# One tile instead of four in the engine loop of two delta-rule layers, with single buffers and three copies by ScalarE

## The reference, cut to what matters

```python
q = softmax(q, axis=-1); k = softmax(k, axis=-1); beta = sigmoid(beta)
def step(W, inp):                     # W: (4, 8, 32, 32), zero at first
    qt, kt, vt, bt = inp
    wk    = einsum('bhde,bhe->bhd', W, kt)
    v_new = bt * (vt - wk)
    W     = W + einsum('bhd,bhe->bhde', v_new, kt)
    return W, einsum('bhde,bhe->bhd', W, qt)
```

## Time and profile before

| | |
|---|---|
| median of three runs | 5422.78 us |
| the profiled execution, device time | 5467.1 us |
| its span | 5465.3 us |
| TensorE busy in the span | 4194.9 us (77%) |
| mean granted TensorE clock | 0.82 of full speed |
| fast-weight layer 0, M updates of its loop (L847) | 542.6 to 1125.9 us |

### The profile page before, as it was taken

One profiled execution on the slowest core, in us unless ns is written; L12 is line 12 of the kernel. 1 busy time (PEld: TensorE's weight loads), 2 busy tenths in 40 slices (PEclk: granted clock), 3 DMA queues, 4 the chain that ended last, 5 costly groups with the idle time before them and its releaser, 6 DMA issues. The chain is left out here.

```text
span 5465.3 us, 173116 instructions
## 1 busy us (share of the span) xinstructions
PE 4194.9 (77%) x75148; PEld 2525.7 (46%) x75149; DVE 2689.1 (49%) x5011; ACT 1812.7 (33%) x3259; POOL 877.7 (16%) x2195
## 2 busy tenths in 40 slices
PE   3666666667986666666788887699999999984995
PEld 1235455453435555554245554255454544533663
DVE  3443223233023323332478887378685886852343
ACT  1121111112121111110366665167575775731221
POOL 0000000000000000000155554011111111104012
PEclk7776666667996666666899998799999999995997
DMA  1000000000000000000100000000000000005123
GB/s 41 2 8 4 4 4 4 4 4 18 0 6 4 4 4 4 4 4 5 37 1 1 1 1 1 9 1 0 1 0 1 0 1 1 0 3 210 61 83 101
DMA packets 47696, 88.13 MB, mean 16 GB/s; under 512 B 7120, under 2 KB 38128, under 8 KB 46064
## 3 DMA queue, kind: packets, MB, share of 16 engines
q1 hardware_dynamic: 40944, 61.84, 3.3%
q0 software_dynamic: 6144, 16.79, 0.9%
HBM read 45.05 MB, written 33.55 MB: 14 GB/s over the span
## 5 line engine op out<-in xcount | busy, mean ns | idle before, releaser
L1618 PE MATMUL psum<-hm_ex,hm_mix 128*128 128x512 f32 x1024 | 510.4, 621 | 42.2 <-ACT hm_Aq L1698 38.2
L1684 ACT ACTIVATE hm_ex<-psum,hm_nm 128x1024 f32<-128x1024 f32 x256 | 285.5, 1115 | 297.6 <-DVE hm_nm L1742 297.6
L1752 DVE TENSOR_SCALAR_CACHE_REDUCE hm_plus<-hm_Aq,hm_cbcol,hm_sums 128x1024 f32<-128x1024 f32 x256 | 340.4, 1330 | 0.0
L1618 PEld LDWEIGHTS psum<-hm_ex,hm_mix 128*128 128x128 f32 x1024 | 175.5, 191 | 352.2 <-issue 344.5
L1757 DVE COPY hm_A<-psum 128x1024 f32<-128x1024 f32 x256 | 312.8, 1222 | 51.5 <-PE psum L1627 47.8
L1742 DVE TENSOR_REDUCE hm_nm<-psum 128x1 f32<-128x1024 f32 x256 | 310.9, 1215 | 13.3 <-PE psum L1606 13.3
L1627 PEld LDWEIGHTS psum<-K,hm_Aq 128*128 128x128 f32 x2048 | 236.7, 140 | 149.9 <-issue 145.2
L666 PE MATMUL psum<-fw_w,fw_stage 128*128 128x512 f32 (+1 forms) x512 | 286.8, 697 | 17.7 <-DMA fw_w<-in_slow 16.6
L1689 ACT ACTIVATE hm_junk<-hm_Aq 128x1024 f32<-128x1024 f32 x256 | 270.6, 1057 | 30.3
L1606 PE MATMUL psum<-hm_kt,hm_qd 64*32 64x512 f32 x4096 | 279.8, 605 | 0.0
L1627 PE MATMUL psum<-K,hm_Aq 128*128 128x128 f32 x2048 | 266.6, 273 | 5.6 <-DVE hm_A L1757 5.6
(11 more groups left out here) (360 smaller groups left out, 8207.4 us busy)
## 6 DMA issues: line engine op xcount, KB each, us to landing
ex_rows_in<-ex_zero SPq DMA_DIRECT2D x2, 5120.0 KB, 24.5
ex_xs<-ex_rows_in SPq DMA_DIRECT2D x80, 128.0 KB
ex_rows_out<-ex_ys SPq DMA_DIRECT2D x80, 128.0 KB, 1.7
ex_w<-in_ex_w SPq DMA_DIRECT2D x2, 4096.0 KB
X<-in_x SPq DMA_DIRECT2D x2, 2048.0 KB, 11.0
out_y<-X SPq DMA_DIRECT2D x2, 2048.0 KB, 9.0
ff_w<-in_ff_w SPq DMA_DIRECT2D x2, 1024.0 KB, 5.9
pt_w_proc<-in_pt_proc SPq DMA_DIRECT2D x1, 2048.0 KB, 7.7
```

What stands on the lines that cost most here:

```text
L1618: mm = pe.matmul(bank[4 + c], mix[:, u, :], ex[:, u, 512 * c:512 * c + 512], start=True, stop=True)
L1684: act.activation(ex[:, u, :], flat2(psum[:, 2 * u:2 * u + 2, :]), ACT.Exp, bias=nm[:, u:u + 1], accum_out=rsum[:, u:u + 1]).then_inc(s_ex, 1)
L1752: dve.tensor_scalar(plus[:, :], Aq[:, u, :], cbcol[:, :], sums[:, :], ALU.add, ALU.add, accum_out=sums[:, :]).then_inc(s_run, 1)
```

## The change

The loop passes from four bodies to one: the bodies -1 to 1 are written out, a loop runs the bodies 2 to 30 (29 passes), and the bodies 31 and 32 follow. So that one body fits every tile, each array has a single buffer. Where the next tile overwrites an array before the recurrence of the tile before has read it, ScalarE copies it: `vhc` from `vh`, `qkTc` from `qkT`, `kc` from the key half of `qk`. The recurrence reads the copies. Several waits are added so that no buffer is overwritten too early, and the orders on TensorE and VectorE are altered: the product of the old state with the queries (into bank 6) stands directly behind the first chain product, the mask `loff` moves into `lower`, and `qm`, `z3` and the parts of the softmax are done in another order. All 14 sets, the projection and the transposes of a tile stay.

```diff
-        qk = sb("qk", [P, 4, QKN]); qkT = sb("qkT", [P, 4, 2 * HEADS, STEP])
-        vh = sb("vh", [P, 4, C])
+        qk = sb("qk", [P, QKN]); qkT = sb("qkT", [P, 2 * HEADS, STEP]); vh = sb("vh", [P, C])
+        kc = sb("kc", [P, C]); qkTc = sb("qkTc", [P, 2 * HEADS, STEP]); vhc = sb("vhc", [P, C])
...
-            for i in range(-1, 4):
-                body(i, i % 4, i + 1 < NT, i >= 0, i >= 1)
-            with eng.Fori(1, NT // 4 - 1) as j:
+            for i in range(-1, 2):
+                body(i, i + 1 < NT, i >= 0, i >= 1)
+            with eng.Fori(2, NT - 1) as i:
                 if start:
                     start()
-                for a in range(4):
-                    body(j * 4 + a, a, True, True, True)
+                body(i, True, True, True)
...
-            for i in range(NT - 4, NT + 1):
+            for i in range(NT - 1, NT + 1):
```

On TensorE:

```diff
                     if rc:
                         pe.wait_ge(s_m, r + 1)
+                        pe.wait_ge(s_ct, r + 1)
                         pe.sem_inc(s_go, 1)
-                        chain(lambda n: qkT[:, ra, HEADS + n, :], M, s_th)
+                        chain(lambda n: qkTc[:, HEADS + n, :], M, s_th)
+                        tiles(lambda n: bank[6][:, cols(n)], lambda n: qkTc[:, n, :], of(M), s_rd, stop=False)
...
                     if rc:
-                        if since(r, 1):
-                            pe.wait_ge(s_att, r)
+                        pe.wait_ge(s_u, r + 1)
+                        pe.wait_ge(s_ck, r + 1)
                         pe.sem_inc(s_go, 1)
-                        tiles(lambda n: bank[6][:, cols(n)], lambda n: qkT[:, ra, n, :], of(M), None, stop=False)
-                        pe.wait_ge(s_u, r + 1)
-                        pe.sem_inc(s_go, 1)
-                        tiles(lambda n: bank[5][:, cols(n)], lambda n: qk[:, ra, C + STEP * n:C + STEP * n + STEP],
-                              of(U), s_up)
+                        tiles(lambda n: bank[5][:, cols(n)], lambda n: kc[:, STEP * n:STEP * n + STEP], of(U), s_up)
```

On ScalarE, first behind the copy of `l2`, then behind that of `tt`:

```diff
+                        act.wait_ge(s_qk, i + 1)
+                        if rc:
+                            act.wait_ge(s_u0, r + 1)
+                        act.activation(vhc[:, :], vh[:, :], ACT.Copy).then_inc(s_cv, 1)
+                        if rc:
+                            act.wait_ge(s_rd, r + 1)
+                        act.activation(flat(qkTc[:, :, :]), flat(qkT[:, :, :]), ACT.Copy).then_inc(s_ct, 1)
...
+                        if rc:
+                            act.wait_ge(s_up, r + 1)
+                        act.activation(kc[:, :], qk[:, C:QKN], ACT.Copy).then_inc(s_ck, 1)
```

More of the change, by code:

```diff
@@ L668, in project, with gram @@
                     mm.then_inc(sig, 1)
-                def gram(a):
+                def gram():
                     for n in range(HEADS):
@@ L692, in body @@
                         pe.sem_inc(s_go, 1)
-                        gram(a)
+                        gram()
                     if rc:
@@ L743, in body @@
                             for b in range(B):
-                                mm = pe.matmul(bank[6][rows(b), cols(n)], qm[rows(b), ru, n, :], U[rows(b), n, :],
+                                mm = pe.matmul(bank[6][rows(b), cols(n)], qm[rows(b), n, :], U[rows(b), n, :],
                                                start=False, stop=(n == HEADS - 1))
@@ L750, in body @@
                         pe.sem_inc(s_go, 1)
-                        product(z3[:, a % 2], loff)
+                        product(z3, loff)
                     if rc:
@@ L765, in _, with body @@
             def _(act):
-                def body(i, a, nxt, ch, rc):
+                def body(i, nxt, ch, rc):
                     r = i - 1
@@ L786, in body @@
                         act.wait_ge(s_t, i * 5 + 5)
-                        act.activation(flat(nt[:, a % 2, :, :]), bank[3][:, 0:C], ACT.Copy, scale=-1.0).then_inc(s_nt, 1)
+                        act.activation(flat(nt[:, :, :]), bank[3][:, 0:C], ACT.Copy, scale=-1.0).then_inc(s_nt, 1)
                     if rc:
@@ L815, in softmax, with strengths @@
                     own.done(dve.reciprocal(rs[:, :], sm[:, :]))
+                def strengths(i):
                     dve.wait_ge(s_root, i + 1)
-                    own.mark(dve.tensor_tensor(split(vh[:, a, :]), split(bank[1][:, 0:C]), wide(eb[:, 2, :], HEADS),
+                    if since(i, 1):
+                        dve.wait_ge(s_cv, i)
+                    own.mark(dve.tensor_tensor(split(vh[:, :]), split(bank[1][:, 0:C]), wide(eb[:, 2, :], HEADS),
                                                ALU.mult))
                     own.done(dve.tensor_tensor(rs[:, HEADS:16], rs[:, HEADS:16], eb[:, 2, :], ALU.mult))
-                    own.done(dve.tensor_tensor(groups(qk[:, a, :]), groups(ex[:, :]), wide(rs[:, :], 16), ALU.mult))
-                    dve.transpose(qkT[:, a, :, :].rearrange("p n j -> p (n j)"), qk[:, a, :]).then_inc(s_qk, 1)
+                def softmax(i):
+                    if since(i, 1):
+                        dve.wait_ge(s_ck, i)
+                    own.done(dve.tensor_tensor(groups(qk[:, :]), groups(ex[:, :]), wide(rs[:, :], 16), ALU.mult))
+                    if since(i, 1):
+                        dve.wait_ge(s_ct, i)
+                    dve.transpose(flat(qkT[:, :, :]), qk[:, :]).then_inc(s_qk, 1)
                 def lower(i):
@@ L827, in lower, with mask, second, factor @@
                     dve.tensor_tensor(z1[:, :, :], small(2), l8t[:, :, :], ALU.subtract).then_inc(s_l8, 1)
-                def masks(u):
                     dve.tensor_tensor(loff[:, :, :], pairs[:, :, 1, :], off, ALU.mult).then_inc(s_lo, 1)
[L831 to L837, removed]
+                def mask(i):
+                    if since(i, 1):
+                        dve.wait_ge(s_in, i)
+                    dve.tensor_tensor(qm[:, :, :], pairs[:, :, 0, :], small(3), ALU.mult).then_inc(s_qm, 1)
+                def second(i):
+                    dve.wait_ge(s_t, i * 5 + 2)
+                    dve.tensor_tensor(z2[:, :, :], split(bank[3][:, 0:C]), z1[:, :, :], ALU.add).then_inc(s_z2, 1)
+                def factor(i):
+                    dve.wait_ge(s_t, i * 5 + 4)
+                    dve.tensor_tensor(z3[:, :, :], split(bank[3][:, 0:C]), z2[:, :, :], ALU.add).then_inc(s_z3, 1)
+                def corrected(r):
                     dve.wait_ge(s_th, r + 1)
-                    dve.tensor_tensor(flat(u0[:, :, :]), vh[:, ra, :], bank[4][:, 0:C], ALU.subtract).then_inc(s_u0, 1)
+                    dve.wait_ge(s_cv, r + 1)
+                    dve.tensor_tensor(flat(u0[:, :, :]), vhc[:, :], bank[4][:, 0:C], ALU.subtract).then_inc(s_u0, 1)
                 def solution(r, n, to, sig):
```

45 lines of the change are left out of this document (21 added, 24 removed).

## The result

| | runs | median, us | all, us | profiled execution, us | span, us | granted clock |
|---|---|---|---|---|---|---|
| before, same chip | 4 | 5421.28 | 5417.58 to 5423.65 | 5467.1 | 5465.3 | 0.82 |
| after | 4 | 5602.91 | 5597.08 to 5603.66 | 5603.49 | 5601.2 | 0.815 |

The changed kernel is slower: ratio 1.0333, 95% interval 1.0315 to 1.0351, or +182 us. The forecast was 5700 us in a range of 4900 to 5830: the direction and the mechanism came out, the size was 98 us too large.

What follows compares the result with a forecast made beforehand. Instruction fetching was taken to bound TensorE. Loop bodies at 33.5 us a tile added 129 + 151 = +280 us, copies, waits and order zero: 5423 + 280, about 5700 us; range 4900 to 5830, the forecast's own 5600 to 5830.

Steps and rivals of the forecast that it cites:

- TensorE is bound by fetching its program: In both layers TensorE runs one packet of 256 instructions, then waits for the next, about 3.77 us a packet.
- 1,840 instructions, at least eight blocks, nine places needed, whole body refetched at each pass, nine packets: One-tile loop body on TensorE: 7.2 blocks of code, lying over at least 8, fetched whole at every pass.
- the block fetched ahead drives out the loop's first: At the loop's end, if the chip keeps 8 blocks or fewer and gives up the oldest, the whole body is refetched.
- 33.5 us a tile: Price of one fetched pass of the new loop, chosen between 32.3 and 33.9 us; 967 us for 29 bodies per layer.
- the upper: Pricing of a loop pass by whole packets: 9 packets x 3.77 us = 33.9 us a tile.
- The way by pieces: Lower pricing of a loop pass: six full blocks, two partial blocks and the gap at the pass's end, 32.3 us.
- Before, 838 + 816 us for 29 + 29 bodies: Cost in the old kernel, layers 0 and 1, of the bodies that the new loop will hold.
- The profiled execution lies 44 us above the median: Correction of the total: 5747 us for an execution like the profiled one, about 5700 us for the runs.
- Copies, waits, order at nothing: ScalarE copies (1.39 us a tile), added waits and new orders: zero; bounds 80 us for copies, 25 to 40 for waits.
- Rival A: All 8 blocks of the loop stay, almost no fetches, 15.5 us a tile: -755 us, 4670 us; chance 0.17.
- Rival B: One layer's loop kept (5190 us), or only one block swapped with the one fetched ahead each pass (4930 us); chance 0.09.
- Rival C: No visible change: fetches vanish, but single buffers chain the engines to about 28 us a tile; 0.02 with everything else.

Runs made afterwards that it cites:

- the placement run: Changed kernel plus only TensorE semaphore instructions ahead of the loops (105 and 218), leaving about 45 instructions in the loop's eighth block: 5210.23 us, ratio 0.9665.
- nine-block run: Changed kernel plus semaphore instructions (93 and 218) ahead of the loops, so the unaltered body lies over nine blocks: 5787.19 us, ratio 1.0661.
- the two paired kernels: Changed kernel with six sets, or one set plus semaphore instructions (173 and 218) ahead of the loops, as block-diagonal 64x64 products: 4664.92 us and 4641.05 us.
- the doubled copies: Changed kernel with each of the three ScalarE copies made twice: 5584.27 us, against 5583.91 us for the changed kernel alongside; on another chip ratio 1.0406.

## Why the prediction was right, and where its size was off

- *TensorE is bound by fetching its program:* right. Where packets stop, TensorE goes from a mean granted clock of 0.64 to 1.00 (the 2.4 GHz level throughout) and a tile from 31.6 to 13.6 us. The control is the change of placement alone, which leaves every instruction of the loop as it was and takes packets and time away together.
- *1,840 instructions, at least eight blocks, nine places needed, whole body refetched at each pass, nine packets:* right to the packet: 1,832 and 252 in 28 passes, twice. The step "the block fetched ahead drives out the loop's first" was right for this placement, but I treated the fetch ahead as certain wherever a loop has eight blocks. It depends on how many instructions the last block holds: with 197 and 235 the block behind is fetched in every pass, with 45 in every second, with 20 in 7 of 28. The placement was luck that I had not priced: with the pads of the placement run the forecast of 5700 us would have been wrong by some 490 us, and in its sign.
- *33.5 us a tile:* the mis-sized term. Measured 31.6 and 31.5, so 2 x 58 = 116 us too much, which more than covers the 98. I had two ways and leaned to the upper, nine packets at 3.77 us. It counts the packet behind the branch at full price although its fetch runs beside the last block, and the two partial blocks as whole. The way by pieces gave 32.3: six blocks 22.6 (measured 22.9), first partial block 3.0 (2.76; the terms that I named for it, 2.22 and the 0.43 us of 14 matmuls, are 2.65 and not 3.0), last 2.4 (2.1), branch 4.1 to 4.5 (3.47). The nine-block run shows again that the number of packets alone does not set the price.
- *Before, 838 + 816 us for 29 + 29 bodies:* held. With 31.5 in place of 33.5, and 5 us off in each layer as in the prediction, the sum gives 2 x (29 x 31.5 - 5) - 1654 = +163 us, so 5586 us, 17 below the measured time. The stage behind the two layers starts 170.9 us later, 8 more than that sum; these 8 are not broken down. These rows are its first matmuls, before and after:

```profile
L1050 PE MATMUL psum<-pt_w_in,H x256: 592/592/1222, 2654.2 to 3292.6; 128*128 128x512 f32 x128
```

```profile
L1078 PE MATMUL psum<-pt_w_in,H x256: 592/592/1222, 2825.1 to 3464.3; 128*128 128x512 f32 x128
```

- *The profiled execution lies 44 us above the median:* right to correct for, and the two traces say where. They differ by 135.9 us in span, not 170.9: the last stage's first transposes start 172.7 us later, but from there to the end the span is 37 us shorter (before, then after). It is the same code in both, so most of the 44 us is one slow stage of one execution, and the +182 us of the medians is the better number.

```profile
L1983 PE MATMUL psum<-K,ex_xs x160: 272/273/474, 5021.0 to 5389.6; 128*128 128x128 f32 x160
```

```profile
L2011 PE MATMUL psum<-K,ex_xs x160: 272/273/474, 5193.7 to 5524.6; 128*128 128x128 f32 x160
```

- *Copies, waits, order at nothing:* right. The lines of ACT in the stretch 412.1:1296.2 (busy, mean ns, idle before) show `qkTc` at 619 ns and the two others at 407 and 416, near the 622 and 383 priced from the earlier trace rows, and only `kc` waits, for TensorE's product, in time that the fetches leave over. The waits view of that stretch (total, times, longest) names "issue" for TensorE and none of the copies:

```profile
L776 ACT ACTIVATE fw_qkTc<-fw_qkT 128x512 f32<-128x512 f32 x28 | 17.3, 619 | 0.0
L787 ACT ACTIVATE fw_kc<-fw_qk 128x256 f32<-128x256 f32 x28 | 11.7, 416 | 77.5 <-PE psum L657 77.5
L773 ACT ACTIVATE fw_vhc<-fw_vh 128x256 f32<-128x256 f32 x28 | 11.4, 407 | 0.0
```

```profile
PEld psum L657 <- issue: 345.2, 186, 4.4
...
PE psum L657 <- issue: 277.2, 130, 4.0
```

- *Rival A, the loop kept:* false for this kernel. Its count of 13.8 us a tile without waits was right, 13.6 measured where the loop is kept with all the work; the 1.7 us that I added for waits did not appear. That its 4670 us lies near the 4641 and 4665 us of the two paired kernels is in part luck: the dearer pairs in one and the pads in the other take the place of those waits. *Rival B, kept in part:* no block-by-block keeping was seen in any run, every pass is whole or none; a mix of whole passes, which I had not thought of, gives 5210 us, and its being near this rival's 5190 is chance. *Rival C* falls with the 13.6 us: single buffers chain nothing at 28.

## What to carry to other kernels

Where an engine's idle time says "issue" in the middle of a run of plain instructions, count the instructions between two stops and the instruction packets per pass: if they match, code size is the resource, and here neither copies nor waits mattered. In this program a loop of TensorE over seven blocks of 256 instructions or fewer was kept, one over eight now and then, by where it ends in its last block, and one over nine never. So count the body with its semaphores and look where in a block it starts. Shortening a loop to one that just misses cost more than leaving it long, since the branch's gap comes more often. Price a refetched pass by its pieces, and compare small differences only on one chip in one batch.

## What was not expected of the hardware

- Whether a loop over eight blocks is kept is decided anew in each pass and goes with how much code stands in the last block: a pass has 0 or 9 packets, never a number between, and 9 in 28 passes of 28, 14 of 28 or 7 of 28.
- The granted clock went to 1.00 in the layers once the gaps were gone, so a kept pass gains twice: the stops are gone (3.5 us at the branch and 0.9 to 2.2 us a block), and sets last 0.74 us instead of up to 1.08.
- A 64x64 set of half as many matmuls takes 1.05 us against 0.72 for the 32x32 set, at the same clock.
- The price of a fetched pass differs between runs of the same kernel in different batches by up to 3% (31.6 against 32.4 us in layer 0), more than the doubled copies, which cost nothing.
